# Two neighbouring pieces of attention scores, in rows 0 to 63 and 64 to 127, issued together

## The reference

```
a1: self-attention, 16 heads of 16, operands rounded to 8 bits     scores 256 x 256 a head
a2: the same against the context                                   scores 256 x 77
    then a gated MLP
sa: self-attention, 16 heads of 16, float32                        scores 256 x 256
ca: the same against the context                                   scores 256 x 77
    then a gated MLP
mh: 8 heads of 32 against the normalised context                   scores 256 x 77
    then a projection that drives a recurrence
attention(x, ctx) = softmax(q k^T * scale) v, then the output projection
```

## Time and profile before

| what | value |
|---|---|
| median of 3 runs | 2770.53 us (2768.13 to 2771.28) |
| the profiled execution | 2757.79 us |
| its span, first to last instruction | 2756.1 us |
| mean granted TensorE clock | 0.968 |
| busy: PE, DVE, ACT, POOL | 2553.0, 1791.0, 1349.3, 758.0 us |
| sa `scores`, line 1016 | 1024 records, 117.1 us busy |
| transposed sa, line 1054 | 1024 records, 101.5 us busy |
| ca and mh `scores`, line 1028 | 1536 records, 89.8 us busy |
| transposed mh, lines 1051 and 1052 | 512 records, 67.4 us busy |

### The profile page before, as it was taken

One profiled execution on the slowest core, in us unless ns is written; L12 is line 12 of the kernel. 1 busy time (PEld: TensorE's weight loads), 2 busy tenths in 40 slices (PEclk: granted clock), 3 DMA queues, 4 the chain that ended last, 5 costly groups with the idle time before them and its releaser, 6 DMA issues. The chain is left out here.

```text
span 2756.1 us, 49674 instructions
## 1 busy us (share of the span) xinstructions
PE 2553.0 (93%) x18872; PEld 1932.0 (70%) x18872; DVE 1791.0 (65%) x4143; ACT 1349.3 (49%) x3518; POOL 758.0 (28%) x841
## 2 busy tenths in 40 slices
PE   5899999999999999999999999999999979998886
PEld 4686777777777778777777777777767665665553
DVE  3985576877777777877777878787764430116765
ACT  2644354656464646555565646564543312225554
POOL 3551132323232323323232324232320010003322
PEclk9998999999999999999999999999999999997877
DMA  5320021112121111111111212121110020001100
GB/s 205 59 52 19 1 41 27 33 28 38 27 35 28 36 28 32 27 32 31 28 35 28 39 28 36 26 35 25 28 32 1 6 59 6 1 1 50 35 20 20
DMA packets 222427, 90.78 MB, mean 33 GB/s; under 512 B 205281, under 2 KB 212785, under 8 KB 221425
## 3 DMA queue, kind: packets, MB, share of 16 engines
q1 hardware_dynamic: 215728, 67.68, 12.5%
q10 hardware_dynamic: 6464, 19.93, 1.9%
HBM read 27.80 MB, written 9.44 MB: 14 GB/s over the span
## 5 line engine op out<-in xcount | busy, mean ns | idle before, releaser
L1122 PE MATMUL psum<-hT,w_l 128*128 128x256 f32 x2048 | 469.6, 383 | 1.9 <-ACT hT L1458 1.9
L1122 PEld LDWEIGHTS psum<-hT,w_l 128*128 128x128 f32 x2048 | 380.6, 190 | 68.3 <-issue 13.6
L1598 ACT ACTIVATE work<-psum 128x1024 f32<-128x1024 f32 (+1 forms) x224 | 220.1, 1021 | 253.8 <-PE psum L1052 127.7
L842 POOL TENSOR_TENSOR rstd<-ms,half 128x2 f32<-128x2 f32 (+1 forms) x144 | 102.5, 712 | 714.3 <-DVE ms L1215 587.5
L1582 ACT ACTIVATE work<-psum,nbias,qs 128x256 f32<-128x256 f32 x512 | 281.4, 570 | 30.8 <-DVE nbias L1294 30.4
L1156 PE MATMUL psum<-w_l 128*128 128x128 f32 x1668 | 247.9, 287 | 3.9 <-ACT bqs L1442 3.7
L1156 PEld LDWEIGHTS psum<-w_l 128*128 128x128 f32 x1668 | 216.0, 194 | 35.3 <-issue 25.7
L882 POOL TENSOR_SCALAR work<-work 128x1024 f32<-128x1024 f32 x128 | 134.3, 1049 | 371.4 <-DVE work L1388 356.6
L1291 DVE TENSOR_REDUCE nmax<-psum 128x4 f32<-128x1024 f32 (+1 forms) x192 | 206.4, 1075 | 43.2 <-PE psum L1002 43.2
L947 PE MATMUL psum<-hT,w_l 128*128 128x256 f32 x896 | 215.8, 386 | 14.6 <-ACT hT L1458 14.4
L1134 PE MATMUL psum<-w_l,work 128*128 128x256 f32 x1024 | 227.8, 381 | 1.4 <-DVE work L1419 1.4
(11 more groups left out here) (195 smaller groups left out, 4756.2 us busy)
## 6 DMA issues: line engine op xcount, KB each, us to landing
w_l<-in_w_l ACTq DMA_DIRECT2D x1, 5120.0 KB, 25.6
x_res<-in_x SPq DMA_DIRECT2D x16, 256.0 KB, 2.7
res<-x_res ACTq DMA_DIRECT2D x16, 256.0 KB, 2.3
w_l<-res SPq DMA_DIRECT2D x16, 256.0 KB, 2.7
out<-work ACTq DMA_DIRECT2D x16, 256.0 KB, 2.0
w_l<-in_w_l ACTq DMA_DIRECT2D x1, 3072.0 KB, 13.9
work<-work SPq DMA_TRANSPOSE x192, 3.1
w_l<-in_w_l SPq DMA_DIRECT2D x2, 1024.0 KB, 8.4
```

Of the source, the lines that this page charges most:

```text
L1122: mm = eng.matmul(banks.tile(key)[:, h * TOKENS:(h + 1) * TOKENS], w1[:, k, h, m * P:(m + 1) * P], hT[p][:, k, :], start=(k == 0), stop=(k ...
L1598: eng.activation(pt(n, p)[0:a.kp, :], banks.pair(key)[0:a.kp, :, :].rearrange("p r n -> p (r n)"), ACT.Exp) \
```

## The change

The loop over PE's list now looks at the next step too. Where a piece is followed at once by another piece of the same attention and item on the other half of the rows, with no filler in between and the next planned to start less than 0.06 us after the first one's planned end, the two are issued by one call. That call first waits for the banks of both, then lets the products take turns on four groups of rows instead of two. Each piece still raises its own semaphore, with its last product: the first piece's comes two products ahead of the second's. Order, planned times, banks, fillers and the steps of the other engines stay as they were.

Applied to the order of the kernel before, the rule takes 182 pairs out of 640 pieces: of `scores` 14 pairs in a1, 16 in a2, 42 in sa, 16 in ca and 13 in mh; of `scores_t` 58 in sa, 8 in ca and 15 in mh.

```diff
+    def beside(self, task, then):
+        if then is None or then[0] != task[0] or then[1] is not task[1] or then[3] != task[3] or then[2][-1] == task[2][-1]:
+            return False
+        this, other = ("tensor", *task), ("tensor", *then)
+        return other not in self.idle and self.end[other] - self.us[other] - self.end[this] < 0.06
...
-                def soft_scores(a, part, p):
-                    half, tile, i = part
-                    key = ("s", a.name, part, p)
-                    ready(key, (kT_ready, (a.name, p)), (q_ready, (a.name, p)))
-                    s = banks.pair(key)
+                def soft_scores(a, parts, p):
+                    for part in parts:
+                        ready(("s", a.name, part, p), (kT_ready, (a.name, p)), (q_ready, (a.name, p)))
                     if a is SA:
                         for j in range(2):
-                            for r in range(2):
...
+                            for half, tile, i in parts:
+                                key = ("s", a.name, (half, tile, i), p)
+                                for r in range(2):
+                                    g = slice(64 * i + 32 * r, 64 * i + 32 * r + 32)
...
+                                if j:
+                                    mm.then_inc(*banks.filled(key))
...
-                def scores_t(a, part, p):
-                    half, kt, i = part
-                    key = ("st", a.name, half, kt, i, p)
-                    ready(key, (shifted, (a.name, half, p)))
+                def scores_t(a, parts, p):
+                    for half, kt, i in parts:
+                        ready(("st", a.name, half, kt, i, p), (shifted, (a.name, half, p)))
                     for j in range(2):
-                        for r in range(2):
...
+                        if a is MH:
+                            for half, kt, i in parts:
+                                for r in range(2):
+                                    g = slice(64 * i + 32 * r, 64 * i + 32 * r + 32)
+                                    eng.matmul(banks.pair(("st", a.name, half, kt, i, p))[0:a.kp, r, j * TOKENS:(j + 1) * TOKENS],
+                                               kc[g, p % STREAMS, j, :], qT(p)[g, j], start=True, stop=False)
+                        for half, kt, i in parts:
...
-                for kind, a, n, p in ORDER["tensor"]:
-                    if ("tensor", kind, a, n, p) in PLAN.idle:
+                done = None
+                for task, then in zip(ORDER["tensor"], ORDER["tensor"][1:] + [None]):
+                    if task == done:
+                        continue
+                    kind, a, n, p = task
+                    if ("tensor", *task) in PLAN.idle:
                         keep_busy(*PLAN.idle["tensor", kind, a, n, p])
-                    steps[kind](a, n, p)
+                    if kind in ("scores", "scores_t"):
+                        done = then if PLAN.beside(task, then) else None
+                        steps[kind](a, [n] if done is None else [n, then[2]], p)
+                    else:
+                        steps[kind](a, n, p)
```

More of the change, by code:

```diff
@@ L987, in values, with scores @@
                            (hT_ready, (a.ln, p)))
-                def scores(a, u, p):
+                def scores(a, parts, p):
                     if not a.quant:
[L991 to L997, removed]
-                        for j in range(2):
-                            for r in range(2):
[L1000 to L1004, removed]
@@ L1006, in soft_scores @@
-                def soft_scores(a, part, p):
-                    half, tile, i = part
-                    key = ("s", a.name, part, p)
-                    ready(key, (kT_ready, (a.name, p)), (q_ready, (a.name, p)))
-                    s = banks.pair(key)
+                        return soft_scores(a, parts, p)
+                    for u, i in parts:
+                        ready(("s", a.name, u, i, p), (kbd_ready, (a.name, p)), *([] if u or i else [(qB_ready, (a.name, p))]))
+                    k = kB(a, p).rearrange("p j (f n) -> p j f n", f=KT)
@@ new lines, in scores @@
+                    for q in range(1 if a is A1 else TT):
+                        for j in range(2):
+                            for u, i in parts:
+                                ft, qt = a.units[u] if a is A1 else (a.units[u][0], q)
+                                for r in range(2):
+                                    g = slice(64 * i + 32 * r, 64 * i + 32 * r + 32)
+                                    c = (2 * q + j) * a.nk
+                                    mm = eng.matmul(banks.pair(("s", a.name, u, i, p))[:, r, c:c + a.nk],
+                                                    tiles(qB(p), KT)[g, ft, qt * P:(qt + 1) * P], k[g, j, ft, :],
+                                                    start=True, stop=True)
+                                if q == (0 if a is A1 else TT - 1) and j:
+                                    mm.then_inc(*banks.filled(("s", a.name, u, i, p)))
@@ L1012, in soft_scores @@
+                def soft_scores(a, parts, p):
+                    for part in parts:
+                        ready(("s", a.name, part, p), (kT_ready, (a.name, p)), (q_ready, (a.name, p)))
                     if a is SA:
                         for j in range(2):
-                            for r in range(2):
[L1015 to L1021, removed]
+                            for half, tile, i in parts:
+                                key = ("s", a.name, (half, tile, i), p)
+                                for r in range(2):
+                                    g = slice(64 * i + 32 * r, 64 * i + 32 * r + 32)
+                                    mm = eng.matmul(banks.pair(key)[:, r, j * TOKENS:(j + 1) * TOKENS],
+                                                    qx(p)[g, 1 - j, half, tile * P:(tile + 1) * P], kx(a, p)[g, 1 - j, half, :],
+                                                    start=True, stop=True)
+                                if j:
+                                    mm.then_inc(*banks.filled(key))
+                        return
+                    for qt in range(TT):
+                        for j in range(2):
+                            for half, tile, i in parts:
+                                key = ("s", a.name, (half, tile, i), p)
@@ L1027, in soft_scores @@
                                         c, q, k = j * TT + qt, qT(p)[g, j], kc[g, p % STREAMS, j, :]
-                                    mm = eng.matmul(s[:, r, c * CTX:(c + 1) * CTX], q[:, qt * P:(qt + 1) * P], k,
+                                    mm = eng.matmul(banks.pair(key)[:, r, c * CTX:(c + 1) * CTX], q[:, qt * P:(qt + 1) * P], k,
                                                     start=True, stop=True)
-                    mm.then_inc(*banks.filled(key))
+                                if qt == TT - 1 and j:
+                                    mm.then_inc(*banks.filled(key))
                 def turn_max(a, half, p):
@@ L1039, in turn_max @@
                     mm.then_inc(*banks.filled(key))
-                def scores_t(a, part, p):
-                    half, kt, i = part
-                    key = ("st", a.name, half, kt, i, p)
-                    ready(key, (shifted, (a.name, half, p)))
-                    s = banks.pair(key)
-                    for j in range(2):
[L1047 to L1056, removed]
+                def scores_t(a, parts, p):
+                    for half, kt, i in parts:
+                        ready(("st", a.name, half, kt, i, p), (shifted, (a.name, half, p)))
+                    for j in range(2):
+                        if a is MH:
+                            for half, kt, i in parts:
+                                for r in range(2):
+                                    g = slice(64 * i + 32 * r, 64 * i + 32 * r + 32)
+                                    eng.matmul(banks.pair(("st", a.name, half, kt, i, p))[0:a.kp, r, j * TOKENS:(j + 1) * TOKENS],
+                                               kc[g, p % STREAMS, j, :], qT(p)[g, j], start=True, stop=False)
+                        for half, kt, i in parts:
+                            key = ("st", a.name, half, kt, i, p)
+                            for r in range(2):
+                                g = slice(64 * i + 32 * r, 64 * i + 32 * r + 32)
+                                out = banks.pair(key)[0:a.kp, r, j * TOKENS:(j + 1) * TOKENS]
+                                if a is MH:
+                                    mm = eng.matmul(out, sel[g, :], tn(p)[g, j, :], start=False, stop=True)
+                                else:
+                                    mm = eng.matmul(out, kx(a, p)[g, j, half, kt * P:kt * P + a.kp], qx(p)[g, j, half, :],
+                                                    start=True, stop=True)
+                            if j:
+                                mm.then_inc(*banks.filled(key))
@@ L1156, in keep_busy @@
```

(12 more changed lines are left out.)

## The result

| | kernel before | changed kernel |
|---|---|---|
| median | 2768.79 us (8 runs, 2751.06 to 2771.28) | 2781.34 us (8 runs, 2772.60 to 2784.08) |
| ratio, 95% interval | | 1.0052 [1.0028, 1.0076] |
| the profiled execution, its span | 2757.79, 2756.1 us | 2781.46, 2779.7 us |
| mean granted clock | 0.968 | 0.966 |

What follows compares the result with a forecast made beforehand. PE, busy 93% of the span, bounds the first three layers with its list plus waits. mh +15.1, transposed sa +0.8, order of products -1.5 give +14.4 us on 2770.5: 2785 us, 8 in 10 for 2764 to 2799.

Steps and rivals of the forecast that it cites:

- the first and last items: Two items more have mh pairs, one of them only the transposed one; at the smaller price 1.9 us together.
- Steps 1 to 4: One item's mh chain: scores start together at 964.45, DVE moves 0.71 us, the transposed pair starts at 970.09 instead of 968.62.
- Step 5: Transposed mh pair: ACT gets the first piece at 972.11, takes 2.02 us for both; `weigh` starts +1.50 us later.
- step 2: mh's scores: DVE reads i=0 where it read i=1 before, so every later DVE step moves by 0.71 us.
- step 4: Transposed mh: the first piece loses its head start; the pair waits for i=1's bank and starts at 970.09 instead of 968.62.
- The split of the 11 items: mh: 5 items at +1.50 us, 6 where the clock falls at +0.95 us, 13.2 us in all.
- step 3: Behind mh's scores: `turn_max`, next sa maxima and `shift` move 0.71 us; the sa pair at 967.11 starts at 968.39.
- The transposed sa pairs: 28 pairs with a late second bank: +0.8 us on PE; ACT's idle 0.57 us covers the first piece's later exponential.
- The order of products: Both banks free: 0 in sa and a1, small savings in ca and a2; -1.5 us taken between 0 and -3.9.
- clock falls as well: Rival: longer idle time ahead of late pairs adds a fall at each of 28 transposed sa places, 23 us, 2808; chance 0.12.
- Packing pays: Rival: late readers have slack and PE keeps savings in ca, a2 and transposed mh, 17 us, so 2754; chance 0.12.
- Done already: Rival: free-bank pairs already run side by side, late ones meet waits there anyway; no change, 2770 (+-4); chance 0.18.

Runs made afterwards that it cites:

- the free pairs: Against the kernel before, only pairs whose second bank is free in its trace are issued together (a1, a2, ca, some sa): 0.9992 [0.9973, 1.0012].

## Why the prediction was right, and where its working was not

The time, the sign and the place are as forecast, and so is the mechanism at mh. That the time is met so closely is in part luck (the first and last items, below). Point by point:

- **Steps 1 to 4** hold to within 0.03 us in the item of the table. **Step 5** is 0.14 us short of it: +1.36 instead of +1.50 at `weigh`, because ACT's two exponentials took 1.93 us (2.02 before) and `weigh` followed sooner.
- **"Nothing behind `weigh` makes this up"** was too strong. Of the 1.36 us an item keeps 1.16. The two parts are 0.63 us for step 2 (0.71 forecast) and 0.55 for step 4 (0.77), each measured alone; their sum is 1.18, against 1.26 for both together without the other pairs.
- **The split of the 11 items** did not hold. I let the short falls of the earlier trace rows stay in six items, at +0.95 us there. In the first trace of the changed kernel only one fall of the ten items from the third on lies at mh (6.8 us, from 713.1), and two stand elsewhere; in its second trace seven lie at mh, three of 3.4 us and four of 6.8. An item with a fall of 3.4 us at mh took 129.9 to 130.2 us before and takes 130.6 now; one with 6.8 takes 131.7 to 131.8. So the falls moved and some got longer, which the sum did not have. The mean of the ten items from the third on rose from 129.78 to 130.63 (130.91 in the second trace), 0.85 to 1.13 us, times 11 some 9 to 12 us against 13.2.
- **The late pairs of sa's scores** have no term of their own; step 3 followed one of them, the sa pair at 967.11. Their waits grew from 2.1 us to 12.7, and in the kernel with all pairs but mh's (8.2 us, 15 times) an item takes 0.24 us more than before, where the free pairs alone (129.02) and the transposed sa pairs alone (128.95) add nothing. No run has them alone.
- **The transposed sa pairs** cost PE 23.6 us more of waiting for ACT (33.4 against 9.8 in the earlier trace rows) and the kernel nothing. From the first of the four exponentials to the end of the last, ACT needs 996.22 + 2.13 - 993.88 = 4.47 us, and in the earlier trace rows 985.63 + 1.02 - 982.20 = 4.45. The gap of 0.57 us took it, as the step said, and the kernel with these pairs alone stands at 0.9997.
- **The order of products** was priced at -1.5 us with an end at nothing; nothing is what the run of the free pairs shows. The ca triple did get shorter (2.01 us instead of the 2.15 of the earlier trace rows; 1.98 to 2.12 was the estimate), and the kernel's time doesn't show it. Most of PE's 46 us are of another kind, at pairs whose second bank is late: one wait ahead of both pieces stands in place of two pieces one after the other. In transposed sa 22.6 us less of busy time stand against 23.6 us more of waiting, and with only the free pairs these pieces stay at 101.9 us busy. The Trainium skill's rule of strictly ordered matmuls ("TensorE: Matmul & The Clock Gate", "Part 3: Packing small matmuls"), by which the sa pairs would have won an estimated 110 us, does not show here: the measurement, 0.9992, decides.
- **The first and last items** were given 1.9 us. Against the first of the two later traces of before, whose last part is equally long (501.6 and 501.8 us), the changed kernel loses 5.0 us up to the first item's line 1143, wins 9.2 in items 1 and 2, loses 9.0 in items 3 to 12 and 7.4 in items 13 to 15, and 0.2 behind. In the 9.2 lies the fall at 448 us, which the changed kernel hasn't. In items 13 to 15 it has three falls, 13.7 us at half clock, where before has none; its second trace has one of 3.4 us there, and loses 1.9 us. Against the profiled execution of before, which hasn't the fall at 448 us either, the spans differ by 23.6 us. So that the total is this near is in part luck: two things that I did not have in the sum stood against each other, dearer ends and a fall that before has in two of its three traces.
- **The rival "clock falls as well"** was right about the danger and wrong about the place. The late sa pairs kept the clock: between 230 and 2250 us no fall begins within 20 us behind a late transposed one, in both traces of the changed kernel and in that with these pairs alone. Mh's pair would have lost the clock in most items, had its products stayed in the old order (the kernel with only the waits). **"Packing pays"** fell with the changed kernel, though two partial versions end on its side (0.9969 and 0.9971), by the clock and not by PE's savings. **"Done already"** holds for the 154 pairs outside mh in the kernel's time (1.0006), and nearly so in the middle items (+0.24 us).

What stays open is when the fall at 448 us comes. It is there in the two later traces of before and in those of the kernels with only the free pairs, only the sa pairs and only mh's scores, where that item's mh pieces start between 443.6 and 445.0 us. It is missing in the profiled before (443.9) and with mh's pairs alone (444.4), and in every kernel in which they start at 446.4 us or later. So the gain of the two faster versions may hang on when an item arrives, and not on its pairs as such; no run here settles it. The traces speak for it: with mh's transposed pairs, and with these and the free pairs, the last item's line 1143 starts 4.4 and 2.1 us later than in the profiled before, and 7.0 and 9.3 us earlier than in the first of the two traces with the fall.

## What to carry to other kernels

Work that is issued as a pair waits for the later of its two operands: before pairing, read which of them is late now, what the early one was doing in the meantime (a head start for its reader can be worth more than the engine's saving), and which reader starts on the first result. A falling busy share of the busiest engine proves no gain; measure from one fixed row per item to the next, and take the items with a fall of the clock apart. And when a new wait stands on TensorE, test it once with filler work in the gap, since the granted clock can cost more than the wait.

## What the hardware showed that I had not expected

- **Pieces on different groups of rows overlap without taking turns.** Sixteen records of two sa pieces in the old order last 1.16 us, in turns 1.15.
- **A busy engine can stand at the lower clock level.** In the kernel with only the waits PE is busy for 25.64 of 26 us at a granted clock of 0.54, after 1.37 us of idle time and a pair in the old order. After 1.41 us and the same products in turn on four groups it was granted 1.00 over 26 us; with 1.60 us of filler products in the gap it was 1.00 as well, over the 6 us shown. One such fall lasts 23.9 us and costs an item 10 to 11 us.
- **Turns on four groups are no safeguard.** The kernel with only mh's scores in turns still shows falls of 23.9 us at 447 and 717 us and of 13.7 us at 857 us.
- **One fall is half of the spread** of the kernel before: 11.0 us of the 20 between its shortest and longest runs.
